# An embedding tower kernel: its first period gathered, turned, listed and contracted in two halves of 32 samples

## The chip, the core and the metric

The kernel runs on one core of a Trainium2 chip. The core has a matrix engine (TensorE, here PE, with a queue of its own for weight loads, PEld), a vector engine (VectorE, DVE), a scalar engine (ScalarE, ACT), GpSimd (POOL) and a queue engine for transfers (SyncE, SP). They run on their own instruction streams and meet at semaphores. The metric is the time of one execution on the device in microseconds (us).

## What is computed

For each of 1024 samples, 32 rows of 16 numbers are looked up in 32 tables (`x0`, fields m, components d). Three layers of a compressed interaction network follow, then a small dense tower:

```python
x0 = embeddings                      # [b, m, d], m = 32 fields, d = 16
xk = x0
outs = []
for W in (W0, W1, W2):               # W: [32, h, 64]
    xk = relu(einsum('bmd,bhd,mhk->bkd', x0, xk, W))
    outs.append(sum(xk, axis=2))
z = concatenate(outs, axis=1)        # [b, 192]
h = concatenate([z, dense_ctx], axis=1)
h = maximum(h @ W_top1 + b_top1, 0)
h = maximum(h @ W_top2 + b_top2, 0)
y = h @ W_top3
```

All numbers are fp32.

## The kernel before

**Tiles.** The batch is cut into 16 periods of 64 samples. A period has 64 x 16 = 1024 columns, cut into two streams of 512 columns (`s = 2q` and `2q + 1` of period q, the upper half of d in the second). Layers 1 and 2 multiply every field with every channel of the layer below: per stream and layer 16 steps of 128 rows, made in 4 units of 4 steps (`half` 0 or 1, `u` 0 or 1). A unit is one DVE product of 128x2048 (`outer` in `vector`, L555): rows of listed fields times the stream's relu'd sums, which lie in PSUM as `x1a`/`x1b` (layer 1) or `x2a`/`x2b` (layer 2; a for half 0, b for half 1). There are 32 streams x 2 layers x 4 = 256 units. PE contracts a unit against `w1` or `w2` into `acca` or `accb`. The products go through a ring of five buffers (`RING`), so unit n waits until unit n - 5 is contracted (`s_used`).

**Slots.** `streams(j)` names what shares slot j: slot 0 has layer 1 of streams 0 and 1, slot j layer 1 of stream j + 1 and layer 2 of stream j - 1. PE (`outer`, L639) contracts two units at a time, one in each half of its columns, into the two halves of one PSUM bank; `vector_units(j)` is DVE's order of the eight units.

**How a period comes in.** GpSimd gathers 16 times 128 table rows (`gather`, L417) into `emb`, two buffers in turn. PE turns them into `spread` (`turn_fields`, L599), ACT copies them to the 32 partitions of `field` (`fields_out`, L778), and SP writes 30 copies of groups of eight fields, in a fixed pattern, to `field_dram` (`list_fields`, L318, five transfers, pieces of 2 KB). From there SP reads `mates` (L326), for later periods `across` and `squares`, and `rows` (L346): partition p of tile t holds field number p + t of the list.

**Layer 0.** For periods 0 and 1 DVE makes five products of 128x1024 (`product0`, L536) into `prod0`, which has four places, so the fifth waits for PE's first contraction. From period 2 on GpSimd makes four (L435) and ACT squares the fields. PE contracts them into `acc0` (`layer0`, L605, L619); `SUM0` says after which pair (slot, i) that stands in PE's order. ACT copies `acc0` twice into `x1a` (`input1`, L783) and, with halves exchanged, in four pieces into `x1b` (L789); `input2` does so for `x2a` and `x2b` from the sums of layer 1. `z1`, `z2`, `z3` (L795) write relu'd sums for the reduction over d, which GpSimd does (`halve12`, `halve3`, L439 to L445).

**Fillers.** `keep_busy` (L612) issues matmuls whose result is not used, in front of PE work that follows a wait.

**What sets the order.** All orders are written by hand, one per engine: `FIELDS_AT`, `SUM0` and `TOWER_AT` place turnings, layer 0 and the dense tower between pairs on PE, and `stretches(q)` cuts GpSimd's gathers by how far PE has come.

## Time and profile before

| | |
|---|---|
| median of 3 runs | 638.52 us (638.24 to 638.60) |
| profiled execution, its own time | 638.18 us |
| its span in the trace | 636.4 us |
| DVE busy | 579.8 us |
| PE busy | 584.7 us |
| GpSimd busy | 444.7 us |
| ACT busy | 366.3 us |

The span runs from the first to the last instruction of the profiled execution; 1.8 us of its own time lie outside it. A timeline row gives start and duration of merged instructions of one kind and, in brackets, the idle time before them and what ended it. Intervals of DVE and ACT in a row of several are their union. Each fp32 matmul of the code appears as two records. In the chain that ended last DVE's `outer` has 51% of the span and PE's contraction of pairs 17%.

### The profile page before, as it was taken

The numbers are of one execution on the slowest core, as the hardware profiler recorded it, in microseconds if no ns is written. First come the engines' busy times: TensorE is split into PE (matmuls) and PEld (weight loads), VectorE is DVE, ScalarE is ACT, GpSimd is POOL, SyncE is SP. The second block draws the span as 40 slices with busy tenths as digits, with TensorE's granted clock in tenths as the row PEclk, the third lists the DMA queues.
The fourth block names the chain that finished last, engine by engine and source line by source line (L and its number), as shares of the span: only waits on it lengthen the run. The fifth ranks groups of instructions, "written<-read, shape, count | busy, mean of one in ns | idle before, by whom it ended". The sixth has DMA issues, their size and how long they took to land.

```text
span 636.4 us, 7868 instructions
## 1 busy us (share of the span) xinstructions
PE 584.7 (92%) x2896; PEld 209.6 (33%) x2896; DVE 579.8 (91%) x309; ACT 366.3 (58%) x607; POOL 444.7 (70%) x416
## 2 busy tenths in 40 slices
PE   0078899999898989999999999999999999999998
PEld 0023233333232323333334323333334323334355
DVE  1039899999999999999999999999999999999995
ACT  0006474767656565747676575747676575737551
POOL 6677787698888878886979688886989582703012
PEclk9999999999999999999999999999999999999999
DMA  6296598938293845749291846648391946600000
GB/s 172 46 323 143 231 231 257 326 64 295 73 262 129 220 188 123 286 75 334 49 302 62 222 185 147 263 95 314 59 320 38 238 166 150 257 4 1 1 2 1
DMA packets 31315, 105.83 MB, mean 166 GB/s; under 512 B 8774, under 2 KB 14028, under 8 KB 27052
## 3 DMA queue, kind: packets, MB, share of 16 engines
q1 hardware_dynamic: 23084, 103.21, 51.6%
q0 software_dynamic: 8192, 2.11, 2.5%
q8 instruction: 23, 0.38, 0.2%
q14 instruction: 16, 0.13, 0.1%
HBM read 89.56 MB, written 15.73 MB: 165 GB/s over the span
## 4 chain that ended last, share of the span: by engine, by line
DVE 52%; PE 26%; issue 12%; DMA 5%; POOL 2%; SPq 1%; ACT 1%; DVEq 0%; ACTq 0%
DVE prod L555 51%; PE accb L648 9%; PE acca L648 8%; DMA rows<-field_dram 3%; POOL emb L417 2%; PE spread L691 2%; PE acc L605 2%; DMA field_dram<-zb_field 1%; PE accb L669 1%; PE acc L669 1%; SPq L318 1%; DVE prod L536 1%; PE spread L686 1%; ACT zb_field L778 0%; PE spread L612 0%
## 5 line engine op out<-in xcount | busy, mean ns | idle before, releaser
L417 POOL DMA_INDIRECT emb<-in_table,idx x256 | 246.4, 963 | 79.8 <-issue 67.8
L648 PE MATMUL acca<-prod,w 128*64 128x512 f32 x1024 | 229.1, 594 | 2.5 <-DVE prod L555 1.7
L648 PE MATMUL accb<-prod,w 128*64 128x512 f32 x960 | 216.1, 596 | 10.6 <-DVE prod L555 10.6
L555 DVE TENSOR_TENSOR prod<-rows,x1a 128x2048 f32<-128x2048 f32 x64 | 145.7, 2278 | 4.9 <-ACT x1a L783 2.5
L555 DVE TENSOR_TENSOR prod<-rows,x1b 128x2048 f32<-128x2048 f32 (+1 forms) x65 | 145.7, 2245 | 2.0 <-PE accb L648 1.4
L555 DVE TENSOR_TENSOR prod<-rows,x2a 128x2048 f32<-128x2048 f32 x64 | 145.6, 2278 | 0.8 <-PE accb L648 0.8
L555 DVE TENSOR_TENSOR prod<-rows,x2b 128x2048 f32<-128x2048 f32 x64 | 145.6, 2277 | 0.0
L648 PEld LDWEIGHTS acca<-prod,w 128*64 128x64 f32 x1024 | 71.7, 137 | 144.6 <-issue 134.3
L648 PEld LDWEIGHTS accb<-prod,w 128*64 128x64 f32 x960 | 65.8, 137 | 153.0 <-issue 113.7
L435 POOL TENSOR_TENSOR prod<-rows,mates 128x1024 f32<-128x1024 f32 x42 | 99.3, 2382 | 6.8 <-DMA rows<-field_dram 6.6
L783 ACT ACTIVATE x1a<-acc 64x512 f32<-64x512 f32 x62 | 35.3, 570 | 114.6 <-PE acc L605 113.9
L439 POOL TENSOR_TENSOR zin<-zin 128x512 f32<-128x512 f32 (+1 forms) x24 | 30.5, 1270 | 74.4 <-ACT zin L795 74.1
L789 ACT ACTIVATE x1b<-acc 32x512 f32<-32x512 f32 x124 | 69.9, 564 | 5.3 <-DVE prod L555 3.5
L605 PE MATMUL acc<-prod,w 128*64 128x512 f32 x248 | 59.0, 594 | 0.3 <-DVE prod L536 0.2
L789 ACT ACTIVATE x2b<-acca 32x512 f32<-32x512 f32 x64 | 36.0, 563 | 21.7 <-DVE prod L555 21.1
L795 ACT ACTIVATE zin<-accb 64x512 f32<-64x512 f32 (+1 forms) x32 | 33.0, 1032 | 26.0 <-PE accb L648 22.8
L536 DVE TENSOR_TENSOR prod<-rows,mates 128x1024 f32<-128x1024 f32 x10 | 11.7, 1223 | 36.4 <-DMA rows<-field_dram 34.7
L795 ACT ACTIVATE zin<-acca 64x512 f32<-64x512 f32 x32 | 33.8, 1056 | 15.0 <-PE acca L648 14.6
L435 POOL TENSOR_TENSOR prod<-across,mates 128x1024 f32<-128x1024 f32 x14 | 33.3, 2381 | 12.8 <-issue 12.5
L778 ACT ACTIVATE zb_field<-spread 32x256 f32<-32x256 f32 x64 | 23.9, 374 | 25.0 <-PE spread L599 24.1
L599 PE MATMUL spread<-ident,emb 128*32 128x128 f32 x256 | 11.2, 294 | 26.2 <-DMA emb<-in_table,idx 26.2
L789 ACT ACTIVATE x2b<-accb 32x512 f32<-32x512 f32 x60 | 33.8, 562 | 0.9
(84 smaller groups left out, 309.3 us busy)
## 6 DMA issues: line engine op xcount, KB each, us to landing
rows<-field_dram SPq DMA_DIRECT2D x30, 2048.0 KB, 11.9
field_dram<-zb_field SPq DMA_DIRECT2D x32, 256.0 KB
mates<-field_dram SPq DMA_DIRECT2D x16, 512.0 KB, 4.4
across<-field_dram SPq DMA_DIRECT2D x56, 128.0 KB, 4.5
emb<-in_table,idx POOLq DMA_INDIRECT x256
field_dram<-zb_field SPq DMA_DIRECT2D x32, 128.0 KB
field_dram<-zb_field SPq DMA_DIRECT2D x16, 192.0 KB
rows<-field_dram SPq DMA_DIRECT2D x2, 1024.0 KB, 7.1
```

The costliest lines, as they stand in the source:

```text
L417: pool.indirect_dma_start(out=emb[q % EMBS][:, j * EMB:(j + 1) * EMB], out_offset=None, in_=table, in_offset=bass.IndirectOffsetOnAxis(ap= ...
L435: nc.gpsimd.tensor_tensor(prod0[:, k, :], other, mates[:, :], ALU.mult).then_inc(s_prod0p, 1)
L439: nc.gpsimd.tensor_tensor(by_d[:, :, 0:DH], by_d[:, :, 0:DH], by_d[:, :, DH:EMB], ALU.add).then_inc(s_eight, 1)
L536: nc.vector.tensor_tensor(prod0[:, place0(q, k), :], rows[:, slot(q, t), :], mates[:, :], ALU.mult).then_inc(s_prod0v, 1)
L555: nc.vector.tensor_tensor(prod[:, n % RING, t:t + count, :], rows[:, at + t:at + t + count, c * HALF:(c + 1) * HALF], xs, ALU.mult).then_i ...
L605: mm = nc.tensor.matmul(to[c * HID:(c + 1) * HID, :], w, operand[:, c * HALF:(c + 1) * HALF], start=first, stop=last)
L648: mm = nc.tensor.matmul(acc[j % 2][side * HID:(side + 1) * HID, :], (w1 if layer == 1 else w2)[:, step, :], prod[:, (made(layer, s, half, ...
L669: mm = nc.tensor.matmul(sums_alone(s)[c * HID:(c + 1) * HID, 0:PART], w2[:, step, :], prod[:, n % RING, i, c * PART:(c + 1) * PART], start ...
L778: last = nc.scalar.activation(by_d[:, d, :, :, :], turned[d * FIELDS:(d + 1) * FIELDS, :, :, :], ACT.Copy)
L783: last = nc.scalar.activation(to[h * HID:(h + 1) * HID, :], src, ACT.Relu)
L789: last = nc.scalar.activation(to[block * FIELDS:(block + 1) * FIELDS, :], src[of:of + FIELDS, :], ACT.Relu)
L795: return nc.scalar.activation(by_d[:, c * count:(c + 1) * count, :], src.rearrange("k (d b) -> k d b", b=BT), ACT.Relu)
```

## The change

Period 0 is processed as two halves of 32 samples; h is the half. The ids of period 0 are laid out on the host so that the first 8 gathers bring all fields of samples 0 to 31 and the next 8 those of samples 32 to 63. GpSimd issues the second 8 after the first turning.

- `turn_first(h)`, `fields_first(h)`, `list_first(h)`, `mates_first(h)`, `rows_of_half(h, g)` do per half what was done once. A half's list has the same 30 copies in 8 transfers of 3 or 4 copies each (`EIGHTS`), in pieces of 128 numbers (512 B); 4 are issued by SP and 4 by ACT.
- A stream of period 0 is now one half of the samples with all 16 d, still 512 columns. `product_first(h, k)` makes products of 128x512, `layer0_first` contracts them in pieces of 256 columns.
- The 16 units of period 0 (`FIRST_UNITS`) are contracted one stream at a time (`outer_alone`, eight matmuls of 256 columns), in this order, two units per name: (1,0) half 0, (1,0) half 1, (2,0) half 0, (1,1) half 0, (1,1) half 1, (2,0) half 1, (2,1) half 0, (2,1) half 1, where (layer, stream). The products of half 1's layer 0 stand after the first four.
- ACT's copies for period 0 go by 256 columns: `split_twice` has 4 instructions (before 2), `split_changed_over` 8 (before 4), `split_by_d` 2 per half.
- Slots 0 and 1 are gone. The products of period 1 follow the 16 units, then slot 2 holds layer 1 of streams 2 and 3, and slot 3 has the order that slot 1 had. Layer 0 of period 2 follows the last pair of slot 2 (before, after pairs 0 and 1 of it); that of period 3 stands one pair later in slot 4.
- The first add of table bases to the ids covers period 0 alone, a second the other periods.

```diff
+    FIRST = [(0, 2), (2, 3), (5, 3)]
+    FIRST_SLOT = 2
+    FIRST_UNITS = ([(1, 0, half, u) for half in range(2) for u in range(UNITS)] +
+                   [(2, 0, 0, u) for u in range(UNITS)] +
+                   [(1, 1, half, u) for half in range(2) for u in range(UNITS)] +
+                   [(2, 0, 1, u) for u in range(UNITS)] +
+                   [(2, 1, half, u) for half in range(2) for u in range(UNITS)])
...
-    for q in range(2, PERIODS):
-        SUM0[2 * q - 2, 0] = [(k, q) for k in range(3)]
-        SUM0[2 * q - 2, 1] = [(SQUARES, q), (L0 - 1, q)]
+        late = q == 3
+        SUM0[2 * q - 2, late] = [(k, q) for k in range(3)]
+        SUM0[2 * q - 2, 1 + late] = [(SQUARES, q), (L0 - 1, q)]
...
+        def list_eights(queue, h, odd):
+            for first, of, step, times in EIGHTS[odd::2]:
...
+                queue.dma_start(to, part).then_inc(s_listed_first[h], 16)
...
-            list_fields(0)
-            mates_in(0)
-            for g, (t, count) in enumerate(FIRST):
-                spread_rows(0, t, count, s_first[g])
+            for h in range(SPLITS):
+                list_first(h)
+                mates_first(h)
+                for g in range(len(FIRST)):
+                    rows_of_half(h, g)
...
             pool.wait_ge(s_at, 1)
-            gather_early(0)
-
+            gather(0, 0, FIRST_GATHERS)
             pool.wait_ge(s_turned, 1)
+            pool.wait_ge(s_turned, 1)
+            gather(0, FIRST_GATHERS, FIRST_GATHERS)
+            pool.wait_ge(s_turned, SPLITS)
+            pool.wait_ge(s_at, 2)
             gather_early(1)
...
+                if k >= RING0:
+                    dve.wait_ge(s_l0, h * STEPS0 + k - RING0 + 1)
...
             pe.wait_ge(s_ident, 1)
-            turn_fields(0, 0)
+            turn_first(0)
 
             pe.wait_ge(s_w12, 32)
-            pe.wait_ge(s_listed, len(LIST_PARTS) * 16)
-            keep_busy(acc[1][:, :], 5)
+            pe.wait_ge(s_listed_first[0], len(EIGHTS) * 16)
+            keep_busy(acc[1][:, :], 2)
+            turn_first(1)
+            keep_busy(acc[1][:, :], 2)
             pe.wait_ge(s_w0sum, 3)
-            for k in order0(0):
-                layer0(k, 0)
-            turn_fields(1, 0)
-
+            for k in range(EARLY):
+                layer0_first(k, 0)
+            for i, unit in enumerate(FIRST_UNITS):
+                outer_alone(*unit)
+                if i == 2 * UNITS - 1:
+                    for k in range(EARLY):
+                        layer0_first(k, 1)
+                if i == 3 * UNITS - 1:
+                    turn_fields(1, 0)
+            turn_fields(2, 0)
+            for k in order0(1):
+                layer0(k, 1)
...
+            fields_first(0)
+            fields_first(1)
+            first_input(1, 0, 0)
+            first_input(1, 0, 1)
+            first_z(0, 0)
+            first_input(2, 0, 0)
+            first_input(2, 0, 1)
+            first_input(1, 1, 0)
+            first_z(1, 0)
+            first_input(1, 1, 1)
             fields_out(1)
```

DVE's order at the start. `prod0<-rows,mates` are products of layer 0, `prod<-rows,x..` units of layers 1 and 2. Before:

```order
L536 TENSOR_TENSOR prod0<-rows,mates 128x1024 x5
L555 TENSOR_TENSOR prod<-rows,x1a 128x2048
L555 TENSOR_TENSOR prod<-rows,x2a 128x2048
L555 TENSOR_TENSOR prod<-rows,x1a 128x2048
L555 TENSOR_TENSOR prod<-rows,x2a 128x2048
L555 TENSOR_TENSOR prod<-rows,x1b 128x2048
L555 TENSOR_TENSOR prod<-rows,x2b 128x2048
L555 TENSOR_TENSOR prod<-rows,x1b 128x2048
L555 TENSOR_TENSOR prod<-rows,x2b 128x2048
L536 TENSOR_TENSOR prod0<-rows,mates 128x1024 x5
L555 TENSOR_TENSOR prod<-rows,x2a 128x2048 x2
```

And now:

```order
L603 TENSOR_TENSOR prod0<-rows,mates 128x512 x5
L638 TENSOR_TENSOR prod<-rows,x1a 128x2048 x2
L638 TENSOR_TENSOR prod<-rows,x1b 128x2048 x2
L603 TENSOR_TENSOR prod0<-rows,mates 128x512 x5
L638 TENSOR_TENSOR prod<-rows,x1a 128x2048 x2
L638 TENSOR_TENSOR prod<-rows,x2a 128x2048 x2
L638 TENSOR_TENSOR prod<-rows,x2b 128x2048 x2
L638 TENSOR_TENSOR prod<-rows,x1b 128x2048 x2
L638 TENSOR_TENSOR prod<-rows,x2a 128x2048 x2
L638 TENSOR_TENSOR prod<-rows,x2b 128x2048 x2
L612 TENSOR_TENSOR prod0<-rows,mates 128x1024 x5
L638 TENSOR_TENSOR prod<-rows,x1a 128x2048
```

The products of period 1 moved from behind 8 units to behind 16, and layer 1 of streams 2 and 3 (slot 2) follows them, where before layer 2 of stream 0 (slot 1) did.

PE's order in slot 4 and the start of slot 5, where layer 0 of period 3 stands (`acc<-prod,w` and `acc<-squares,w`; a pair is `acca` or `accb` x8; `spread<-ident,emb` is the turning of period 4). Before:

```order
L599 MATMUL spread<-ident,emb 32x128 x8
L648 MATMUL acca<-prod,w 64x512 x8
L605 MATMUL acc<-prod,w 64x512 x6
L648 MATMUL acca<-prod,w 64x512 x8
L619 MATMUL acc<-squares,w 64x512 x2
L605 MATMUL acc<-prod,w 64x512 x2
L648 MATMUL acca<-prod,w 64x512 x16
L648 MATMUL accb<-prod,w 64x512 x32
```

And now:

```order
L684 MATMUL spread<-ident,emb 32x128 x8
L759 MATMUL acca<-prod,w 64x512 x16
L700 MATMUL acc<-prod,w 64x512 x6
L759 MATMUL acca<-prod,w 64x512 x8
L730 MATMUL acc<-squares,w 64x512 x2
L700 MATMUL acc<-prod,w 64x512 x2
L759 MATMUL acca<-prod,w 64x512 x8
L759 MATMUL accb<-prod,w 64x512 x32
```

One more pair (x8) stands ahead of the layer 0 products, and one pair fewer behind them.

ACT's order at the start, now, with `x1a<-acc` the first input of layer 1 and `DMA field_dram<-zb_field` its share of the listing (before, ACT issued no transfer):

```order
L907 ACTIVATE zb_field<-spread 32x4x32 x4
L339 DMA field_dram<-zb_field 32x4x128 x2
L339 DMA field_dram<-zb_field 32x3x128
L339 DMA field_dram<-zb_field 32x4x128
L907 ACTIVATE zb_field<-spread 32x4x32 x4
L339 DMA field_dram<-zb_field 32x4x128 x2
L339 DMA field_dram<-zb_field 32x3x128
L339 DMA field_dram<-zb_field 32x4x128
L915 ACTIVATE x1a<-acc 64x256 x4
```

Both halves' copies and eight transfers stand ahead of the first `x1a`, where one set of copies did.

## Rows read from the trace of the kernel before

**Rows 1.** Page, part 1: busy us, instructions; part 2: granted clock, 40 slices, tenths.

```profile
PE 584.7 (92%) x2896; PEld 209.6 (33%) x2896; DVE 579.8 (91%) x309; ACT 366.3 (58%) x607; POOL 444.7 (70%) x416
...
PEclk9999999999999999999999999999999999999999
```

**Rows 2.** Timeline of DVE: start us, us, line, operation, count [idle before].

```profile
40.87 5.98 DVE L536 TENSOR_TENSOR prod<-rows,mates 128x1024 f32<-128x1024 f32 x5 [33.95 <-DMA rows<-field_dram]
49.32 2.29 DVE L555 TENSOR_TENSOR prod<-rows,x1a 128x2048 f32<-128x2048 f32 x1 [2.46 <-ACT x1a L783]
51.52 2.28 DVE L555 TENSOR_TENSOR prod<-rows,x2a 128x2048 f32<-128x2048 f32 x1
...
68.58 4.63 DVE L536 TENSOR_TENSOR prod<-rows,mates 128x1024 f32<-128x1024 f32 x4 [1.59 <-issue]
74.00 1.22 DVE L536 TENSOR_TENSOR prod<-rows,mates 128x1024 f32<-128x1024 f32 x1 [0.79 <-DMA rows<-field_dram]
```

**Rows 3.** Timeline of GpSimd (POOL), 0 to 100 us.

```profile
3.67 1.12 POOL L417 DMA_INDIRECT emb<-in_table,idx  x1 [2.20 <-DVE idx L514]
...
22.59 0.94 POOL L417 DMA_INDIRECT emb<-in_table,idx  x1 [0.30 <-issue]
26.32 0.94 POOL L417 DMA_INDIRECT emb<-in_table,idx  x1 [2.79 <-PE spread L599]
...
98.37 7.07 POOL L435 TENSOR_TENSOR prod<-rows,mates 128x1024 f32<-128x1024 f32 x3 [2.88 <-DMA rows<-field_dram]
```

**Rows 4.** Timeline of PE, 0 to 50 us.

```profile
24.94 1.09 PE L599 MATMUL spread<-ident,emb 128*32 128x128 f32 x16 [24.94 <-DMA emb<-in_table,idx]
34.46 7.04 PE L612 MATMUL accb<-w 128*128 128x512 f32 x10 [8.44 <-DMA field_dram<-zb_field]
...
49.87 4.56 PE L612 MATMUL accb<-w 128*128 128x512 f32 x10
```

**Rows 5.** Timeline of ACT, 20 to 75 us.

```profile
26.08 1.53 ACT L778 ACTIVATE zb_field<-spread 32x256 f32<-32x256 f32 x4 [24.05 <-PE spread L599]
48.04 1.15 ACT L783 ACTIVATE x1a<-acc 64x512 f32<-64x512 f32 x2 [20.43 <-PE acc L605]
...
70.79 1.15 ACT L783 ACTIVATE x2a<-acca 64x512 f32<-64x512 f32 x2 [12.10 <-PE acca L648]
```

**Rows 6.** Timeline of SP's queue, 25 to 55 us.

```profile
27.63 3.90 SPq L318 DMA_DIRECT2D field_dram<-zb_field  x5
34.34 0.34 SPq L326 DMA_DIRECT2D mates<-field_dram  x1
...
51.95 3.88 SPq L318 DMA_DIRECT2D field_dram<-zb_field  x5
```

**Rows 7.** DMA, 28.5 to 30.5 us: queue: packets, MB, share of 16 engines' time.

```profile
q1 hardware_dynamic: 210, 0.40, 99.6%
```

**Rows 8.** Page, part 3: queue, packets, MB, share of 16 engines' span.

```profile
q0 software_dynamic: 8192, 2.11, 2.5%
```

**Rows 9.** DMA, 34.5 to 47 us: totals.

```profile
DMA packets 896, 4.49 MB, mean 360 GB/s; under 512 B 167, under 2 KB 279, under 8 KB 535
```

**Rows 10.** Groups by shape, 560 to 637 us: xcount | busy, mean ns.

```profile
L669 PE MATMUL accb<-prod,w 128*64 128x256 f32 x64 | 7.3, 381 | 0.0
...
L795 ACT ACTIVATE zin<-accb 64x256 f32<-64x256 f32 x2 | 1.2, 610 | 2.8 <-PE accb L669 2.8
```

**Rows 11.** Timeline of DVE, 75 to 160 us.

```profile
98.80 2.29 DVE L555 TENSOR_TENSOR prod<-rows,x2a 128x2048 f32<-128x2048 f32 x1 [0.84 <-PE accb L648]
...
111.99 2.28 DVE L555 TENSOR_TENSOR prod<-rows,x2a 128x2048 f32<-128x2048 f32 x1
...
151.61 2.28 DVE L555 TENSOR_TENSOR prod<-rows,x2a 128x2048 f32<-128x2048 f32 x1
```

**Rows 12.** Timeline of PE, one pair of units in slot 4.

```profile
140.22 3.60 PE L648 MATMUL acca<-prod,w 128*64 128x512 f32 x16
```

**Rows 13.** Timeline of ACT, 140 to 150 us.

```profile
145.65 1.15 ACT L783 ACTIVATE x1a<-acc 64x512 f32<-64x512 f32 x2 [6.64 <-PE acc L605]
```

More of the change, by code:

```diff
@@ L70, in cin_tower_kernel @@
     BLOCKS = P // FIELDS
+    SPLITS = 2
+    SPLIT = BT // SPLITS
+    FIRST_GATHERS = GATHERS // SPLITS
+    PIECE = QUAD * SPLIT
+    EIGHTS = [(first + e, 2 * half + j // 8 + e, step, times) for j, count, half, first, step, times in LIST_PARTS
+              for e in range(count // 8)]
     GROUPS = [(0, 4), (4, 4)]
-    FIRST = [(0, 2), (2, 2), (4, 1), (5, 3)]
+    FIRST = [(0, 2), (2, 3), (5, 3)]
     BUFFERS = 3
@@ L741, in _ @@
             pe.wait_ge(s_ctx, 16)
-            towers, turned = 0, 2
-            for j in range(SUBS):
+            towers, turned = 0, turned_by(2)
+            for j in range(FIRST_SLOT, SUBS):
                 for i in range(2 * UNITS if j < SUBS - 1 else 4 * UNITS):
@@ L747, in _ @@
                     else:
[L748 to L751 removed]
+                        outer_alone(*vector_units(j)[i])
                     if (j, i) in TOWER_AT:
@@ L779, in fields_out, with fields_first @@
                 last.then_inc(s_field, 1)
+            def fields_first(h):
+                act.wait_ge(s_turned, h + 1)
+                by_d = field[:, h * HALF:(h + 1) * HALF].rearrange("n (f d b) -> n d f b", f=BLOCKS, b=SPLIT)
+                turned = spread[:, h * P:(h + 1) * P].rearrange("q (f b) -> q f b", b=SPLIT)
+                for d in range(QUAD):
+                    last = nc.scalar.activation(by_d[:, d, :, :], turned[d * FIELDS:(d + 1) * FIELDS, :, :], ACT.Copy)
+                last.then_inc(s_field, 1)
+                act.wait_ge(s_field, h + 1)
+                list_eights(act, h, 1)
@@ new lines, in split_by_d, with layer0_half @@
+            def split_by_d(to, of, h, done):
+                by_d = to.rearrange("k (b d) -> k d b", d=EMB)
+                for c in range(2):
+                    last = nc.scalar.activation(by_d[:, c * DH:(c + 1) * DH, h * SPLIT:(h + 1) * SPLIT],
+                                                of[c * HID:(c + 1) * HID, :].rearrange("k (d b) -> k d b", b=SPLIT), ACT.Relu)
+                last.then_inc(done, 1)
+            def layer0_half(h):
+                return acc0[:, h * PART:(h + 1) * PART]
```

317 lines of the change are left out of this document (218 added, 99 removed).

## The prediction

> **What bounds the kernel now.** I read the page first: DVE is busy for 579.8 us of the 636.4 us span and PE for 584.7 us [rows 1]. In steady state one `outer` unit starts 2.20 us after the one before it (49.32 to 51.52) [rows 2], and there are 256 of them, which makes 563 us. A pair of units costs PE 3.60 us [rows 12] against 4.40 us on DVE, so DVE sets the pace. What an edit at the start can bring is therefore the idle time of DVE before and between its first units. The timeline of DVE shows it: nothing until 40.87 us, five products of layer 0, 2.46 us of waiting for `x1a`, the eight units of slot 0, then the products of period 1 at 68.58 us, the last of which waits for rows until 74.00 us [rows 2].
>
> The timelines of the other engines show what the first 40.87 us are made of, in series: 16 gathers from 3.67 to 22.59 us, 1.26 us apart [rows 3]; 2.35 us from the start of the last to the turning on PE, which takes 1.09 us [rows 4]; four copies by ACT, 1.53 us [rows 5]; the listing, 27.63 to 34.34 us [rows 6]; then 6.5 us until mates and the first rows are in [rows 2, 6]. The change attacks this series.
>
> **What comes earlier: half 0.** Eight gathers at 1.26 us put the eighth at 12.5 us, and 2.35 us later PE turns it: 14.8 us. It has half the matmuls, so half of 1.09 us: 15.4 us. ACT then copies 32x128 pieces in place of 32x256 (383 ns each) [rows 5]; between half of that and all of it I take 0.31 us, four of them 1.3 us: 16.7 us.
>
> The listing of a half is 960 pieces of 512 B in place of 480 of 2 KB for the whole. The wire time is the unknown. In the listing of before, 210 packets fill 16 engines to 99.6% for 2 us, so one takes 152 ns, and the rate is 0.2 MB per us [rows 7]. If bytes decide, 0.49 MB take 2.5 us. If each piece costs what a packet of 2 KB does, 960 x 152 / 16 = 9.1 us. The gathers' packets of about 258 B cost 2.5% of 16 x 636.4 us over 8192 packets, 31 ns each [rows 8], which is far nearer the first. I take 3.0 us. The listing of before has 6.7 us from issue to mates, of which 0.98 MB at that rate are 4.9 us, so 1.8 us lie around it: a half lands 4.8 us after its fields, at 21.5 us. Two issuing queues, SP's and ACT's, are not counted as a gain, since the engines were full.
>
> That full wire agrees with the Trainium skill, DMA: Bandwidth & Descriptors, Rules for kernel authors: spreading transfers over SP, ACT and GpSimd doesn't add bandwidth and only saves issue time. The same page's Specifications give 512 B as the smallest transfer at line rate; by that the pieces would take the 2.5 us and the sum would be 0.5 us better, and no run here shows pieces of 512 B from SBUF yet.
>
> Mates and first rows are half the bytes: 0.75 MB less at 360 GB/s [rows 9] is 2.1 us off the 6.5 us: 25.9 us, against 40.87 us.
>
> **What holds half 0 back again: half 1.** PE's queue has `turn_first(1)` and two groups of two `keep_busy` matmuls ahead of the first contraction. GpSimd's second eight gathers start only after the first turning: 15.4 + 0.3 = 15.7 us, the eighth at 24.5 us, turned at 26.8 to 27.4 us. The second `keep_busy` pair takes 1.8 us at the rate of the later group (4.56 us for five) [rows 4]; the first group ran five in 7.04 us, and its slow ones are at half that rate [rows 4], which would make a pair 3.6 us. The granted clock is listed as full (9, 90% or more) in every slice [rows 1], so the durations are what I go by. PE idles from 25 to 27 us here, so either is possible. The fifth product of layer 0 waits for the first contraction (`prod0` has four places). So contractions end at 31.4 us at the fast rate and 33.9 us at the slow one; I take 32.4 us, between them.
>
> ACT splits each field by 256 columns: four `ACTIVATE` at 383 ns [rows 5] are 1.6 us for `x1a` (1.15 us before), and eight are 3.1 us for `x1b` (2.3 us before). So `x1a` is ready at 34.0 us and the first unit starts at 34.1 us, 15.2 us earlier than 49.32 us. ACT's own four DMA issues of half 1 lie at 28.7 us to 30.5 us (SP's first ones of before take about 0.4 us, all five 3.90 us because the wire was full [rows 6]), before it is needed.
>
> **From there to period 1.** DVE runs 4 units (34.1 to 42.9), five half products (3.0 us; the rows of half 1 would be in at about 37 us, so nothing is waited for), then waits about 0.6 us for layer 2 of half 0: PE ends the fourth unit 1.8 us after it is made (64 records of 128x256 in 7.3 us are four units) [rows 10], and ACT needs 1.6 us. The twelve units left are 26.4 us with 0.2 us of waiting for ACT: 73.1 us. The rows of period 1 don't come earlier in proportion: ACT copies the fields of period 1 only after `first_input(1, 1, 1)`, ending at 56.9 us. From the start of that listing (51.95) to the first product was 16.6 us, to the fifth 22.0 us [rows 2, 6], so 73.6 and 79.0 us; the fifth product ends at 80.3 us. Now 16 units are done where before 8 were (at 75.2 us): 17.6 us of units for 5.1 us.
>
> **What is uncovered.** Two hand-overs that had cover lose it. First, slot 2 starts right after these products, so DVE waits 2.4 us for the last contraction and `x1a`, as it did once before [rows 2]: 82.7 us. Eight units later, at 100.3 us, DVE needs `x2a` of stream (2, 2), for which PE must finish the pair (3.65 us) and ACT copy twice (1.15 us). Before, DVE ended slot 0 at 66.99 us and ACT ended `x2a` at 71.94 us [rows 2, 5], and the products of period 1 lay in that gap. Now nothing does: 4.9 us idle, until 105.2 us. That is unit 25; before it started at 111.99 us [rows 11]. Gain so far 6.8 us.
>
> Then unit order a, a, b, b on slot 3 makes the ring of five wait twice, which before fell into slots 1 and 2 (0.84 us the longer [rows 11]): 1.3 us. Last, layer 0 of period 3 stands one pair later on PE. Before, it ended at 145.6 us and `x1a` at 146.8 us [rows 13], for the second unit of slot 5, which is the one before that at 151.61 us [rows 11] and so starts at 149.4 us: 2.6 us of margin. One pair costs 3.6 us on PE [rows 12]; with the backlog of the wait before it `x1a` comes at 145.8 us where DVE wants it at 143.9 us: 1.9 us. Unit 43 starts at 105.2 + 18 x 2.198 + 1.3 + 1.9 = 148.0 us, before at 151.61 us [rows 11]: 3.6 us. Later slots keep their order, so this stays to the end.
>
> GpSimd is 1.4 us late after gather(1) (27.7 against 26.32 [rows 3]), which doesn't count: its products of period 2 were held by rows until 98.37 us [rows 3], those rows are asked for about 2 us earlier now, so they end near 103.5 us (105.44 before), and PE takes them up from 103.9 us, wanting the last only at 107 us. Extra adds and memsets on DVE (32 memsets took 0.9 us) lie under the gathers.
>
> Sum against the profiled execution: 638.18 - 3.6 = 634.6 us; the median is 0.34 us above it, so 634.9 us.
>
> **Rivals.** (1) *The late pieces don't bite*: `keep_busy` at the fast rate (0.9 us), and period 3's `x1a` in time (1.9 us), wire by bytes (0.5 us): 6.9 us gained, 631.6 us. For it: each term stands on margins of 1 to 2 us. Against: they would all have to fall the same way.
>
> (2) *The head start is eaten*: PE at its slow rate past 27 us (1.5 us more), first units slow as well because PE idles some 4 us before them (0.5 us), and period 1's rows 1 to 2 us later: 3.5 us less, 638.4 us, no change. For it: the group at 34.46 us started slow after idling [rows 4].
>
> (3) *ACT is blocked by its own listing, slower*: if a piece costs 152 ns, half 0 lands at 27.6 us, and PE's turning of half 1 moves behind it to 31.8 us. Half 1's wire takes 9.1 us from 33.1 us, and ACT's four issues are held as SP's were (3.90 us of issuing for 4.9 us of wire [rows 6, 7]), until about 40.4 us; `first_input(1, 0, 0)` is queued behind them. The first unit then starts at 42.0 us, 7.9 us later than forecast: 642.8 us. It turns slower once the first unit starts after 37.7 us, that is at about 110 ns a piece. Against: 31 ns for the gathers' packets.
>
> (4) *The split doesn't advance the first unit*, since everything waits for PE's order: then the first unit would be near 49 us. The sum above would need 15 us of error; it would give some 650 us and has 0.01, counted in (3).
>
> **Numbers.** Forecast 0.60, from 1.3 to 6 us gained. Rival 1 has 0.08, rival 2 0.16, rival 3 with 4 0.16. A measurement of this kernel can tell about 0.2%, 1.3 us, from no change. Faster 0.68, same 0.16, slower 0.16. The range leaves out most of rival 3 and the far end of rival 1: 631.0 to 639.0 us.
>
> **What would show it.** First product of layer 0 at about 26 us and first unit at 34.1 us; period 1's products at 73.6 us with the fifth at 79.0 us; 4.9 us of DVE idle before the first `x2a` unit of slot 3; about 1.9 us before the second unit of slot 5; unit 43 at 148.0 us. I am wrong if a half's listing takes over 6 us, if PE's contractions end after 35 us, or if the products of GpSimd for period 2 or 3 are what PE waits for.

## The result

The changed kernel takes 642.40 us (median of 6 runs, 640.50 to 642.99) beside 638.58 us before (6 runs, 638.24 to 638.93): the ratio is 1.0053 (95% interval 1.0039 to 1.0067). It is slower by 0.5%, where 634.9 us and a gain were forecast. The profiled execution took 640.72 us with a span of 638.8 us, against 638.18 and 636.4 us before.

The granted clock of the changed kernel in 40 slices, in tenths. Before, this line was full throughout [rows 1].

```profile
PEclk9889999899999999999999999999999999999999
```

Timeline of DVE, the changed kernel. It answers to [rows 2, 11]. Units are counted in DVE's order: unit 25 is the first of slot 3, unit 43 the third of slot 5.

```profile
25.10 1.29 DVE L603 TENSOR_TENSOR prod<-rows,mates 128x512 f32<-128x512 f32 x2 [17.60 <-DMA rows<-field_dram]
...
35.84 0.69 DVE L603 TENSOR_TENSOR prod<-rows,mates 128x512 f32<-128x512 f32 x1 [5.11 <-PE acc L721]
39.16 4.49 DVE L638 TENSOR_TENSOR prod<-rows,x1a 128x2048 f32<-128x2048 f32 x2 [2.63 <-ACT x1a L915]
...
78.39 5.87 DVE L612 TENSOR_TENSOR prod<-rows,mates 128x1024 f32<-128x1024 f32 x5
86.87 2.29 DVE L638 TENSOR_TENSOR prod<-rows,x1a 128x2048 f32<-128x2048 f32 x1 [2.61 <-issue]
...
109.48 4.48 DVE L638 TENSOR_TENSOR prod<-rows,x2a 128x2048 f32<-128x2048 f32 x2 [4.94 <-ACT x2a L961]
...
121.62 2.29 DVE L638 TENSOR_TENSOR prod<-rows,x2b 128x2048 f32<-128x2048 f32 x1 [1.06 <-PE accb L759]
125.13 4.49 DVE L638 TENSOR_TENSOR prod<-rows,x1b 128x2048 f32<-128x2048 f32 x2 [1.21 <-PE accb L759]
...
134.60 2.29 DVE L638 TENSOR_TENSOR prod<-rows,x2a 128x2048 f32<-128x2048 f32 x1 [0.60 <-PE accb L759]
...
151.87 2.29 DVE L638 TENSOR_TENSOR prod<-rows,x1a 128x2048 f32<-128x2048 f32 x1 [1.79 <-ACT x1a L961]
154.07 2.28 DVE L638 TENSOR_TENSOR prod<-rows,x2a 128x2048 f32<-128x2048 f32 x1
```

The first product comes 15.8 us earlier than before (25.10 against 40.87), the first unit 10.2 us earlier (39.16 against 49.32), unit 25 is 2.5 us ahead (109.48 against 111.99), and unit 43 is 2.46 us behind (154.07 against 151.61). From there both kernels run alike: 2.4 us is also the difference of the spans (638.8 against 636.4). So everything that decides lies in the first 154 us.

SP's queue and, below it, GpSimd and PE of the changed kernel (start us, us, operation, count, idle before).

```profile
16.51 1.79 SPq L339 DMA_DIRECT2D field_dram<-zb_field  x4
20.84 0.34 SPq L366 DMA_DIRECT2D mates<-field_dram  x1
21.23 1.39 SPq L371 DMA_DIRECT2D rows<-field_dram  x3
```

```profile
24.86 0.94 POOL L470 DMA_INDIRECT emb<-in_table,idx  x1 [0.30 <-issue]
32.21 0.94 POOL L470 DMA_INDIRECT emb<-in_table,idx  x1 [6.40 <-PE spread L694]
```

```profile
20.96 3.68 PE L707 MATMUL accb<-w 128*128 128x512 f32 x4 [5.63 <-DMA field_dram<-zb_field]
31.25 0.67 PE L694 MATMUL spread<-ident,emb 128*32 128x128 f32 x8 [6.61 <-DMA emb<-in_table,idx]
31.84 3.37 PE L707 MATMUL accb<-w 128*128 128x512 f32 x4
...
41.51 8.79 PE L784 MATMUL acca<-prod,w 128*64 128x256 f32 x64 [3.98 <-DVE prod L638]
...
116.23 8.78 PE L759 MATMUL accb<-prod,w 128*64 128x512 f32 x32 [3.69 <-DVE prod L638]
127.47 7.09 PE L759 MATMUL accb<-prod,w 128*64 128x512 f32 x32 [2.46 <-DVE prod L638]
```

The listing of a half is quick, 16.51 to 20.84 us, with the 16 DMA engines busy with its pieces for 84.7% of the time (17 to 20 us: totals, then SP's queue q1 and ACT's q10):

```profile
DMA packets 1059, 0.47 MB, mean 157 GB/s; under 512 B 141, under 2 KB 1059, under 8 KB 1059
...
q1 hardware_dynamic: 544, 0.25, 45.5%
q10 hardware_dynamic: 456, 0.21, 39.2%
```

The rows of half 0 are then asked for at 21.23 us. The last gather of half 1 starts at 24.86 us, near the 24.5 us of the forecast, and is turned only at 31.25 us. The chain of waits gives the time between to that one transfer, and a third of it to the last gather of half 0, beside which no other kind of transfer ran:

```profile
12.38 2.15 DMA emb<-in_table,idx
...
24.86 6.25 DMA emb<-in_table,idx
```

The transfers of 25 to 28 us: totals, then packets, MB and share of 16 engines of SP's queue (q1, the rows) and GpSimd's (q0, the gathers):

```profile
DMA packets 197, 0.95 MB, mean 317 GB/s; under 512 B 25, under 2 KB 44, under 8 KB 197
...
q1 hardware_dynamic: 164, 0.94, 83.4%
q0 software_dynamic: 33, 0.01, 5.6%
```

The rows take most of the engines' time, and the gathers' small packets (q0) trickle among them. Stretches of the changed kernel (busy us and count of PE, PEld, DVE, ACT, POOL, then granted clock, DMA share, GB/s):

```profile
26.00:32.00 6.00, 0.75 (x9) 0.40 (x9) 1.69 (x3) 0.03 (x1) 0.00 (x0) 0.65 0.53 198
32.00:36.00 4.00, 4.00 (x12) 1.65 (x14) 0.16 (x1) 1.04 (x4) 2.88 (x4) 0.67 0.52 94
42.00:46.00 4.00, 4.00 (x26) 2.35 (x24) 4.00 (x3) 1.17 (x2) 3.09 (x4) 0.64 0.71 263
...
116.00:120.00 4.00, 3.77 (x10) 1.18 (x12) 4.00 (x3) 3.89 (x7) 3.09 (x4) 0.57 1.15 227
```

The clock goes to its lower level, 1.2 of 2.4 GHz, around three idle stretches of PE, 24.6 to 31.2 us, 37.5 to 41.5 and 112.5 to 116.2 us: in steps of 2 us the granted clock is 0.50 in every step from 28 to 34 us, at 42 to 44 and at 118 to 120 us. Not every idle stretch is followed by it: behind 2.46 us of idling, at 127.47 us, the clock is full and 32 records take 7.09 us. And the column doesn't show all slow work: the four records at 20.96 us took 3.68 us, twice the 1.8 us of the full rate, with a granted clock of 1.00 in every step from 20 to 26 us. The idle stretch from 112.5 us lies between layer 0 of period 2, now behind the last pair of slot 2, and the first `x2a` unit of slot 3.

### The profile page after: what moved, and what is told of

Its sections match the earlier page's. It is cut to its first block, busy times and chain, and to the rows that moved or that the text cites. A ratio compares the mean times of both kernels' runs of the same rounds, so it can differ in the third digit from the quotient of the medians.

```text
span 638.8 us, 8220 instructions
## 1 busy us (share of the span) xinstructions
PE 581.9 (91%) x3026; PEld 218.3 (34%) x3026; DVE 581.6 (91%) x347; ACT 371.1 (58%) x641; POOL 443.2 (69%) x416
## 4 chain that ended last, share of the span: by engine, by line
DVE 49%; PE 33%; issue 12%; POOL 2%; ACT 2%; DMA 2%; DVEq 1%; ACTq 0%; POOLq 0%
DVE prod L638 49%; PE accb L759 10%; PE acca L759 9%; PE acc L700 3%; PE acca L784 3%; POOL emb L470 2%; PE spread L806 2%; DMA emb<-in_table,idx 1%; PE accb L784 1%; PE acc L784 1%; PE acc L730 1%; PE accb L707 1%; PE spread L801 1%; DVEq L627 0%; ACT x2b L923 0%
## 5 line engine op out<-in xcount | busy, mean ns | idle before, releaser
L759 PE MATMUL acca<-prod,w 128*64 128x512 f32 x960 | 215.0, 594 | 4.1 <-DVE prod L638 3.3
L759 PE MATMUL accb<-prod,w 128*64 128x512 f32 x896 | 203.3, 600 | 15.5 <-DVE prod L638 15.5
L759 PEld LDWEIGHTS acca<-prod,w 128*64 128x64 f32 x960 | 67.2, 137 | 137.0 <-issue 127.0
L759 PEld LDWEIGHTS accb<-prod,w 128*64 128x64 f32 x896 | 61.9, 137 | 149.6 <-issue 107.2
L492 POOL TENSOR_TENSOR zin<-zin 128x512 f32<-128x512 f32 (+1 forms) x24 | 30.5, 1270 | 77.5 <-ACT zin L973 77.2
L967 ACT ACTIVATE x1b<-acc 32x512 f32<-32x512 f32 x116 | 65.4, 564 | 4.7 <-DVE prod L638 3.0
L700 PE MATMUL acc<-prod,w 128*64 128x512 f32 x236 | 55.6, 592 | 0.0
L967 ACT ACTIVATE x2b<-acca 32x512 f32<-32x512 f32 x60 | 33.8, 563 | 16.4 <-DVE prod L638 15.8
L973 ACT ACTIVATE zin<-acc 64x512 f32<-64x512 f32 x30 | 31.8, 1058 | 0.5
L967 ACT ACTIVATE x2b<-accb 32x512 f32<-32x512 f32 x56 | 31.5, 562 | 0.8
L603 DVE TENSOR_TENSOR prod<-rows,mates 128x512 f32<-128x512 f32 x10 | 6.5, 686 | 26.1 <-DMA rows<-field_dram 20.6
```

What stands on the lines that cost most here:

```text
L492: nc.gpsimd.tensor_tensor(by_d[:, :, 0:DH], by_d[:, :, 0:DH], by_d[:, :, DH:EMB], ALU.add).then_inc(s_eight, 1)
L700: mm = nc.tensor.matmul(to[c * HID:(c + 1) * HID, :], w, operand[:, c * HALF:(c + 1) * HALF], start=first, stop=last)
L759: mm = nc.tensor.matmul(acc[j % 2][side * HID:(side + 1) * HID, :], (w1 if layer == 1 else w2)[:, step, :], prod[:, (made(layer, s, half, ...
L967: last = nc.scalar.activation(to[block * FIELDS:(block + 1) * FIELDS, :], src[of:of + FIELDS, :], ACT.Relu)
L973: return nc.scalar.activation(by_d[:, c * count:(c + 1) * count, :], src.rearrange("k (d b) -> k d b", b=BT), ACT.Relu)
```

## The experiments

All ratios are to the kernel before, run on the same chip beside it.

**Theory.** The rows of half 0 delay the last gather of half 1 by 4 us; PE's clock after its idle stretches costs 1.6 us at the start and more in slots 3 and 4; and layer 0 of period 3 costs 1.8 us in slot 5. **Rivals:** GpSimd's waits for the turnings delay it; PE's order alone does; or GpSimd's late gathers of period 1 do.

### The changed kernel again

> The changed kernel once more, unchanged. Theory A (PE's clock falls in three idle stretches, and how long it stays low depends on the moment at which the stretch falls): the time is again between 640.5 and 643.0 us, and this profile shows the same three stretches under full clock (about 26 to 36 us, 42 to 46 us, 116 to 120 us), with durations that differ by some tenths to 2 us. Theory B (the scatter of 2 us between runs comes from the transfers at the start): the first unit on DVE starts at another time than 39.16 us while the clock columns stay the same.

641.15 us (5 runs, 640.61 to 645.47), ratio 1.0043 (1.0029 to 1.0058). The profiled execution was the slowest one, 645.47 us, which is 2.5 us above the range expected, and so shows what scatters. Timelines of DVE and PE in it (the last row of PE, as in a later profile too, counts only the records up to the end of the window asked for):

```profile
85.16 1.23 DVE L612 TENSOR_TENSOR prod<-rows,mates 128x1024 f32<-128x1024 f32 x1 [1.85 <-DMA rows<-field_dram]
...
124.75 2.29 DVE L638 TENSOR_TENSOR prod<-rows,x2b 128x2048 f32<-128x2048 f32 x1 [2.18 <-PE accb L759]
```

```profile
118.22 9.90 PE L759 MATMUL accb<-prod,w 128*64 128x512 f32 x32 [3.69 <-DVE prod L638]
130.59 4.92 PE L759 MATMUL accb<-prod,w 128*64 128x512 f32 x14 [2.46 <-DVE prod L638]
```

The first unit is at 39.26 us, as in the other profile. The 4.7 us between the two executions are 1.85 us of rows of period 1 that came late, and 5.6 us of ring waits (2.18 + 1.21 + 1.13 + 1.08) in place of 2.9: the first 32 records of slot 3 take 9.90 us, or 8.78 in the other profile, and the next 32, behind the 2.46 us of idling, are slow here too (granted clock 0.50 at 132 to 134 us) where they ran at the full rate in the other.

### Rows of half 0 held back

```diff
                 for g in range(len(FIRST)):
+                    if (h, g) == (0, 1):
+                        sp.wait_ge(s_turned, SPLITS)
                     rows_of_half(h, g)
```

> SP issues row groups 2 and 3 of half 0 only after half 1 is turned; nothing else differs. Theory A (the gathers of half 1 land late, 6.4 us after the last issue in place of 2.3 us, because half 0's rows fill the 16 engines): half 1 is turned at 27 to 28.5 us in place of 31.25 us. Rival (the gather after a wait lands late by itself, whatever else is under way): it is still turned at about 31 us. The first unit does not gain as much, since rows now come later: 35 to 38 us in place of 39.16 us, and the whole 0 to 3 us faster than the changed kernel.

640.61 us (10 runs), ratio 1.0024 (1.0004 to 1.0044). PE's timeline:

```profile
27.61 0.66 PE L696 MATMUL spread<-ident,emb 128*32 128x128 f32 x8 [3.15 <-DMA emb<-in_table,idx]
```

The turning comes at 27.61 us, 3.6 us earlier, and 0.2 to 0.8 us behind the forecast of 26.8 to 27.4. The chain gives 2.35 us to the last gather, from 25.12 us, in place of 6.25. With nothing else changed ahead of it, the rows' traffic is shown to be the cause. The held rows cost part of it again (they made DVE wait 5.83 us, first unit at 37.23 us).

### No waits of GpSimd for the turnings

```diff
             gather(0, 0, FIRST_GATHERS)
-            pool.wait_ge(s_turned, 1)
-            pool.wait_ge(s_turned, 1)
             gather(0, FIRST_GATHERS, FIRST_GATHERS)
-            pool.wait_ge(s_turned, SPLITS)
             pool.wait_ge(s_at, 2)
             gather_early(1)
```

Each half has a semaphore of its own for its gathers here.

> GpSimd waits for no turning in periods 0 and 1: the second eight gathers follow the first at once, and those of period 1 follow them; the halves have semaphores of their own, so that the buffers are safe. Theory A (half 1's gathers land late because they fall into half 0's rows, and they fall there because of the wait of 2.8 us): the last one starts at about 22.3 us in place of 24.86 us, half 1 is turned at 24.7 to 28 us in place of 31.25 us, the first unit starts at 32.5 to 36 us, and GpSimd is 8 us ahead at the gathers of period 1. The kernel is 3 to 5 us faster than the changed one. Rival (the wait was covered, the rows alone decide): turned at 30 us or later, the first unit at 38 to 39 us, under 1.5 us faster.

640.39 us (9 runs), ratio 1.0024 (1.0008 to 1.0040). The sixteen gathers now go out 1.25 us apart without a gap, the last at 22.63 us, 2.2 us earlier. PE's timeline:

```profile
30.23 0.66 PE L692 MATMUL spread<-ident,emb 128*32 128x128 f32 x8 [5.15 <-DMA emb<-in_table,idx]
```

The turning moves by 1.0 us and the first unit to 38.25 us, as the rival had it. The last gather now takes 7.46 us to land: of the 2.2 us that GpSimd saves, 1.2 us are lost in the same traffic. The wait named in the change is a small part of the cost.

### Only the wait before the gathers of period 1 removed

```diff
             gather(0, FIRST_GATHERS, FIRST_GATHERS)
-            pool.wait_ge(s_turned, SPLITS)
```

> Only the wait of GpSimd for the second turning is gone; period 1's gathers start at 26.1 us in place of 32.2 us. Theory A (GpSimd is not what the end waits for in the changed kernel): unit 25 still starts at 109 to 110 us, time within 0.5 us of the changed kernel. Rival (the lateness of 6 us on GpSimd is what eats the head start): period 1's rows and the later products come sooner and the kernel is 2 us or more faster.

644.21 us (3 runs, 642.95 to 644.95), ratio 1.0083 (1.0062 to 1.0103): no gain. The first unit is at 39.06 us and the turning at 31.18 us, as in the changed kernel, and the profile is like the slower one of the changed kernel (rows of period 1 late by 1.92 us, ring waits of 5.4 us). The expectation, within 0.5 us of the changed kernel, was missed by more than 1 us on the slow side; the run's interval overlaps the changed kernel's first (1.0039 to 1.0067) and not the second (1.0029 to 1.0058), so with three runs a real loss is not settled. SP asks for the listing of period 1 at 61.84 us here and at 61.95 us in the changed kernel. So GpSimd, 5.9 us late at `gather_early(1)` (32.21 against 26.32 [rows 3]), is not what the end waits for in this order.

### PE kept busy until half 1 is there

```diff
-            keep_busy(acc[1][:, :], 2)
+            keep_busy(acc[1][:, :], 8)
             turn_first(1)
```

> Eight keep_busy matmuls in place of two ahead of the turning of half 1, where PE idled for 6.6 us. Theory A (PE came out of that idle time at half rate): the two after the turning take 1.8 us in place of 3.4 us, contractions follow at 33.7 us in place of 35.1 us, first unit at about 37.6 us, and the kernel is 1.0 to 1.6 us faster than the changed one. Rival (the rate there does not matter since rows or the fifth product decide): first unit unchanged at 39.2 us.

639.02 us (10 runs, 637.46 to 641.77), ratio 1.0016 (1.0001 to 1.0032). PE's timeline:

```profile
21.14 9.09 PE L707 MATMUL accb<-w 128*128 128x512 f32 x16 [5.45 <-DMA field_dram<-zb_field]
30.74 0.46 PE L694 MATMUL spread<-ident,emb 128*32 128x128 f32 x8 [0.51 <-DMA emb<-in_table,idx]
31.13 1.98 PE L707 MATMUL accb<-w 128*128 128x512 f32 x4
```

The turning is nearly as late as ever, but the four records behind it take 1.98 us in place of 3.37, and the first unit starts at 37.06 us, 2.1 us earlier. Of these, 0.5 us are the turning itself, as this execution's last gather landed in 5.38 us; 1.6 us are what the slow records and the slow turning behind the idle stretch cost.

### Half 1 turned behind the contraction of half 0

```diff
-            keep_busy(acc[1][:, :], 2)
-            turn_first(1)
-            keep_busy(acc[1][:, :], 2)
+            keep_busy(acc[1][:, :], 4)
             pe.wait_ge(s_w0sum, 3)
             for k in range(EARLY):
                 layer0_first(k, 0)
+            turn_first(1)
...
             fields_first(0)
-            fields_first(1)
             first_input(1, 0, 0)
+            fields_first(1)
```

> PE turns half 1 behind the contractions of half 0 in place of ahead of them, with the four keep_busy in one group, and ACT copies half 1's fields after the first x1a. Theory A (half 0 was held back by half 1's gathers through PE's order alone): contractions start on their products, the first unit starts at 33 to 34.5 us in place of 39.16 us, and the start of half 1 is not later than before (turned at 31 to 33 us). If all of it stays, the kernel is 4 to 5 us faster than the changed one, 637.5 to 638.5 us. Rival (the rows of half 0, late for the same traffic, decide as well): first unit at 36 us or later.

638.63 us (10 runs), ratio 1.0004 (0.9992 to 1.0016). The first unit starts at 33.35 us, 5.8 us before that of the changed kernel and 0.75 us before the forecast, and slot 3 at 107.47 us, only 2.0 us before it. The time is 2.5 to 3.8 us below the changed kernel's two medians; 4 to 5 us were expected if all of the start stayed. DVE, then PE:

```profile
33.35 4.49 DVE L638 TENSOR_TENSOR prod<-rows,x1a 128x2048 f32<-128x2048 f32 x2 [2.35 <-ACT x1a L914]
39.18 4.49 DVE L638 TENSOR_TENSOR prod<-rows,x1b 128x2048 f32<-128x2048 f32 x2 [1.34 <-ACT x1b L922]
...
80.20 1.23 DVE L612 TENSOR_TENSOR prod<-rows,mates 128x1024 f32<-128x1024 f32 x1 [1.26 <-PE acc L700]
```

```profile
78.40 0.68 PE L684 MATMUL spread<-ident,emb 128*32 128x128 f32 x16 [2.06 <-DMA emb<-in_table,idx]
```

ACT's copies and transfers of half 1 now stand ahead of `x1b` (1.34 us), the rows of half 1 come late (1.15 us), and the turning of period 2, which stands ahead of period 1's contraction in PE's order, waits for GpSimd until 78.40 us. So the fifth product of period 1 waits 1.26 us and `x1a` of slot 2 makes DVE wait 3.43 us in place of 2.61. Here GpSimd's lateness does count, once the start is 6 us faster.

### PE kept busy ahead of slot 3

```diff
                     for k, q in SUM0.get((j, i), []):
                         layer0(k, q)
+                    if (j, i) == (FIRST_SLOT, 3):
+                        pe.wait_ge(s_field, turned)
+                        keep_busy(spread[:, :], 4)
```

> Four keep_busy matmuls behind layer 0 of period 2, where PE idled for 3.7 us ahead of the first pair of slot 3. Theory A (that idle time let PE's clock fall and the slow pairs cost DVE waits at the ring): the clock column is full from 112 to 128 us, the first two pairs take 7.1 us in place of 8.8 us, the waits of DVE in slots 3 and 4 add up to 1.3 us in place of 2.9 us (5.6 us in e1_again), and the kernel is 1.5 to 2.5 us faster than the changed one, with less scatter. Rival (the ring waits come from the unit order alone): no change in them.

640.75 us (9 runs), ratio 1.0031 (1.0017 to 1.0045). PE's timeline and a stretch of this kernel:

```profile
118.76 7.09 PE L759 MATMUL accb<-prod,w 128*64 128x512 f32 x32
128.31 3.97 PE L759 MATMUL accb<-prod,w 128*64 128x512 f32 x10 [2.46 <-DVE prod L638]
```

```profile
128.00:132.00 4.00, 3.69 (x10) 1.15 (x12) 4.00 (x3) 3.38 (x7) 3.69 (x3) 0.57 0.89 346
```

The pairs behind the filled gap run in 7.09 us, at the full rate, but the clock falls again behind the next idle stretch, 2.46 us in the middle of slot 3. The ring waits are 2.8 us, no less than in the first profile of the changed kernel: half of the expectation held. The scatter didn't shrink either (639.28 to 643.12 us).

### Layer 0 of period 3 where it stood

```diff
-        late = q == 3
+        late = False
```

> Layer 0 of period 3 stands where it stood before, after pairs 0 and 1 of slot 4. Theory A (PE's order costs 1.8 us, since x1a of slot 5 comes late): the wait of 1.79 us ahead of the second unit of slot 5 is gone and nothing takes its place, as GpSimd's products end at 136.4 us and pair 0 at 138.7 us; 1.8 us faster than the changed kernel. Rival (GpSimd is late there and PE would wait for it): PE waits in front of layer 0, DVE waits at the ring, gain under 0.5 us.

640.93 us (5 runs, 640.32 to 641.76), ratio 1.0032 (1.0017 to 1.0047). The wait of 1.79 us in slot 5 is gone, and nothing stands in its place. Against the changed kernel the times overlap, but the profile adds up: against that of the changed kernel its first unit is 0.8 us later and its rows of period 1 are 1.85 us late, and yet its span is only 0.5 us longer. The run with the fills, below, sizes it.

### All idle stretches filled

```diff
-            keep_busy(acc[1][:, :], 2)
+            keep_busy(acc[1][:, :], 8)
             turn_first(1)
...
                 layer0_first(k, 0)
+            keep_busy(acc[1][:, :], 4)
...
+                    if (j, i) in ((FIRST_SLOT, 3), (FIRST_SLOT + 1, 1)):
+                        pe.wait_ge(s_field, turned)
+                        keep_busy(spread[:, :], 4 if j == FIRST_SLOT else 3)
```

> All idle stretches of TensorE that the split opened are filled with products on data already there, nothing else is changed: 8 in place of 2 before the turning of half 1, 4 after half 0's contraction, 4 after layer 0 of period 2 in slot 3 and 3 in the middle of the next slot. Theory (behind the late turning, the rest of the loss is TensorE's clock after idle stretches): the turning of half 1 stays at 30.7 to 31.3 us, but the products behind it run at full rate, the first unit starts at 36.5 to 37.1 us, the granted clock is 1.00 from 32 us to the end of slot 4, the ring waits of slots 3 and 4 are together 1.3 to 1.8 us (2.9 and 5.6 in the two profiled runs of the changed kernel), the wait for x1a in slot 5 stays at 1.8, the span is about 635.5 and the time 636.5 to 637.5, with under 1.5 us between the fastest and the slowest. Rival (the scatter comes from DMA landings or the ring itself): ring waits of 2.5 us and more at a full clock, time 639 to 641 and a scatter as before.

638.19 us (10 runs, 637.22 to 638.69), ratio 0.9991 (0.9981 to 1.0001). The granted clock is full in every run, the turning comes at 30.70 us and the first unit at 37.02 us, as expected, and DVE's timeline has ring waits of 1.5 us in slots 3 and 4:

```profile
121.79 4.49 DVE L638 TENSOR_TENSOR prod<-rows,x1b 128x2048 f32<-128x2048 f32 x2 [0.67 <-PE accb L759]
...
131.51 2.29 DVE L638 TENSOR_TENSOR prod<-rows,x2a 128x2048 f32<-128x2048 f32 x1 [0.84 <-PE accb L759]
```

That is the 1.3 us of the forecast, nearly. Six of the eleven runs of the changed kernel took over 642 us; here the slowest took 638.69 and the spread is 1.5 us. The medians are 3.0 and 4.2 us below those of the changed kernel, or 3.3 and 4.0 us by the ratios, and this is what the slow work behind the idle stretches costs. Against the kernel before nothing is gained: the interval holds 1. The time is 0.7 us above what was expected; 0.90 us of waiting for rows of period 1 stand in this profile.

### The fills, with layer 0 of period 3 where it stood

The two edits above together.

> The same fills, and the layer 0 of period 3 placed behind pairs 0 and 1 of its slot, where it stood before the change (it stood behind pairs 1 and 2 in the changed kernel). Theory: the 1.8 us wait for x1a at the start of slot 5 goes and nothing takes its place, so the time is 1.5 to 2 us below that of the fills alone: 634.5 to 635.8. Rival: VectorE meets the ring or the next x2a instead, and the time is that of the fills alone within 0.5 us.

636.40 us (6 runs, 635.10 to 637.39), ratio 0.9965 (0.9953 to 0.9978): 1.8 us less than the fills alone, which is the length of the wait of 1.79 us. The median lies 0.6 us above the expected range, as with the fills alone. DVE's second unit of slot 5 starts without a wait:

```profile
147.18 2.29 DVE L638 TENSOR_TENSOR prod<-rows,x1a 128x2048 f32<-128x2048 f32 x1
```

### All of it, with half 1 turned behind the contraction

The slot fills, layer 0 of period 3 where it stood, the order of "Half 1 turned behind the contraction of half 0" with four fillers behind that turning, and no wait ahead of `gather_early(1)`, the gathers of period 1 (the expectation calls them those of period 2).

> The fills in the slots and the early layer 0 of period 3 again, and half 1 turned only behind the contraction of half 0 (4 filling products behind the turning), its fields copied by ScalarE behind the first x1a, and no wait of GpSimd before the gathers of period 2. Theory: the first unit starts at 33.3 to 33.8 us, some 3 us before that of the fills alone; of it 1.3 us is given back to the wait for x1b, 1.2 to the rows of half 1, and the 3.4 us wait for x1a of slot 2 that stood in the run with the turning behind the contraction shrinks by about 1 us as GpSimd no longer holds the turning of period 2; unit 43 starts at 148 to 149.5 and the time is 633 to 635.5. Rival: the waits for x1b, rows and the fifth product take all that the earlier first unit gives, and the time is that of the fills with the early layer 0 within 0.5 us.

632.62 us (4 runs, 631.79 to 635.80), ratio 0.9918 (0.9888 to 0.9949): faster than both kernels, and 0.4 us below the range expected, as the rows of half 1 made DVE wait for only 0.27 us. DVE:

```profile
33.56 4.49 DVE L637 TENSOR_TENSOR prod<-rows,x1a 128x2048 f32<-128x2048 f32 x2 [2.35 <-ACT x1a L917]
...
82.47 2.29 DVE L637 TENSOR_TENSOR prod<-rows,x1a 128x2048 f32<-128x2048 f32 x1 [2.61 <-ACT x1a L963]
...
105.08 4.49 DVE L637 TENSOR_TENSOR prod<-rows,x2a 128x2048 f32<-128x2048 f32 x2 [4.94 <-ACT x2a L963]
...
146.40 2.28 DVE L637 TENSOR_TENSOR prod<-rows,x2a 128x2048 f32<-128x2048 f32 x1
```

Unit 25 starts at 105.08 us, where the forecast had 105.2, and unit 43 at 146.40 us, 1.6 us ahead of the 148 expected for this run, which is 5.2 us before 151.61 [rows 11]; the spans differ by the same 5.2 us (631.2 against 636.4). The wait for `x1b` remains (1.37 us). The wait of the fifth product of period 1 (1.26 us) is gone, and the one for `x1a` of slot 2 is down from 3.43 us, in the run with the turning behind the contraction, to 2.61 us, with GpSimd no longer held. Which of the four edits gives how much beyond the run before was not taken apart further.

## Why the prediction was wrong

The direction was wrong, and 642.4 us lies outside the range of 631 to 639 us. One of the signs that the prediction named for being wrong came up: PE's contractions ended after 35 us. In its own steps, against the profiled execution of the changed kernel:

| step | forecast | measured |
|---|---|---|
| listing of a half, from its fields | 4.8 us | 16.5 to 20.8, 4.3 us |
| first product | 25.9 | 25.10 |
| half 1 turned | 26.8 to 27.4 | 31.25 |
| four records of `keep_busy` behind it | 1.8 (slow: 3.6) | 3.37 |
| contractions end | 32.4 | 37.5 |
| first unit | 34.1 | 39.16 |
| wait for `x1a` of slot 2 | 2.4 | 2.61 |
| idle before `x2a` of slot 3 | 4.9 | 4.94 |
| unit 25 | 105.2 | 109.48 |
| ring waits in slots 3 and 4 | 1.3 | 2.9 (5.6 in the second profile) |
| late `x1a` of slot 5 | 1.9 | 1.79 |
| unit 43 | 148.0 | 154.07 |

**The step that failed** is the turning of half 1. The prediction put "the eighth at 24.5 us, turned at 26.8 to 27.4 us": it took the 2.35 us between a gather and its turning from rows beside which only gathers ran [rows 3, 4]. The gathers of half 1 land while the rows of half 0 fill the engines, which its own text had at 360 GB/s [rows 9], and the last took 6.25 us. In the seven profiles with these rows under way it took 5.4 to 7.5 us. Holding the rows brought the turning to 27.61 us; starting the gathers 2.2 us earlier brought it only to 30.23. The prediction's rule on the wire agreed with its page and was applied to the listing alone. The Trainium skill, DMA: Bandwidth & Descriptors, Issuing engines are not separate DMA queues, says that transfers of SyncE, ScalarE and GpSimd run on the same 16 engines and interleave with each other; the 6.25 us against 2.15 us agree with it and give it a size.

**The second** is PE's rate. The end of the contractions was put between the fast and the slow rate. A wait of 2 us for half 1 was foreseen and one of 6.6 us came, and the slow rate with it, which the filled start sized at 1.6 us against the full rate. Of these two steps together come the 5.1 us at the first unit; 0.8 us are given back until unit 25, since the rows of period 1 made DVE wait for nothing in this execution. That is in part luck: in the second profile they cost 1.85 us.

**The third** is the ring. "1.3 us" was taken from the pairs of before at the full clock. The prediction saw that layer 0 of period 2 goes behind slot 2 and that DVE idles for 4.9 us before slot 3, but not that PE then idles for 3.7 us there, and for 2.5 us in the middle of slot 3. Slot 3 has slot 1's order now, and before, five and three fillers stood at these two places of slot 1; the change has none there. PE before:

```profile
76.89 4.56 PE L612 MATMUL accb<-w 128*128 128x512 f32 x10
...
88.89 2.84 PE L612 MATMUL spread<-w 128*128 128x512 f32 x6
```

This is 1.6 us here and 4.3 in the second profile; with the gaps filled the ring waits were 1.5 us, near the size that was forecast. Of the 4.7 us between the two profiled executions the ring has 2.7.

The sum closes: 4.3 us at unit 25, 1.6 us of ring, 0.2 us of the rest are the 6.1 us by which unit 43 is late, and 634.6 + 6.1 is 640.7 us, the profiled execution's 640.72. The median is 1.7 us higher, and where that lies is not shown, since no execution near it was profiled: the ring and the rows of period 1 are what differs between the two profiles, but the granted clocks of the six runs, 0.987 to 0.992, don't follow their times.

**What held.** The bytes decide the listing: a half takes 4.3 us, near the forecast, where 9.1 us of wire stood at the other end. The Trainium skill, DMA: Bandwidth & Descriptors, Specifications, gives 512 B as the smallest transfer at line rate; the trace nearly agrees: 157 GB/s from 17 to 20 us, the ramp included, are a fifth less than the 0.2 MB per us of the 2 KB pieces [rows 7], but the engines were busy for 84.7% of it, and a piece took 41 ns of one engine where a quarter of the 152 ns is 38. By an estimate from this, 960 pieces are 2.5 us of wire, and with the forecast's 1.8 us around it the 4.3 us are explained. The prediction's term of 3.0 us was 0.5 us too long. Also right were both uncovered hand-overs, and the late layer 0 of period 3, which the runs with and without it size at 1.8 us. The head start was about as good as the prediction said once the turning was out of the way and the gaps were filled: unit 25 at 105.08 us. The closeness to 105.2 is in part luck: a wait of 1.37 us for `x1b` that the forecast lacked is made up by a first unit 0.5 us earlier and by rows of period 1 that came in time.

**The rivals.** Rival 3 gave 642.8 us, but the time agrees and the mechanism doesn't: a piece costs about 41 ns of one engine, a quarter of the 152 ns, and ACT's four issues took 1.84 us. Rival 2, the head start eaten by PE's slow rate and slow first units, had the right mechanism for part of the loss, at 638.4 us; it had the landing of half 1 in neither its price nor its reasons. It was also to leave no change, and lacked a term for slots 3 and 4. A rival with the gathers behind the rows' traffic was missing, though both its rows were there. The remark on GpSimd held for this order, but not by its reasons: it was late by 5.9 us and not 1.4, the rows of period 2 were asked for 3.8 us later (93.02 against 89.26 us) and not 2 earlier, and its products ended at 109.45 us, not 103.5, which was still in time for PE. With the turning behind the contraction the remark no longer holds.

**What stays open.** Why the rows of period 1 make DVE wait between 0 and 1.9 us, from execution to execution (0, 1.85, 1.92 us in three profiles whose first units start within 0.2 us of each other), was not tried; how much of the scatter at a full clock it is, is not shown. Nor is it known why the same 2.46 us of idling is followed by slow work in some executions and not in others. The time of the last kernel rests on four runs with one of them at 635.8 us.

## What to carry to other kernels

When a loading phase is split so that its second half overlaps the first half's bulk transfers, price each small transfer of the second half at its landing time under that traffic, and put nothing that waits for it ahead of the first half's work on an in-order engine. A change that removes or moves pairs on TensorE also moves its idle stretches: list each idle stretch that it leaves, and fill it or price the work behind it at half the clock. A head start is worth what is left of it at the first point where all orders are again the old ones; compute that point, and check every hand-over that lay under the work that was moved.

## What the runs showed of the hardware

- An indirect gather of 128 rows landed 2.15 us after its start with only gathers under way, and 6.25 us after it with row transfers beside it (317 GB/s in all). Over seven profiles with these rows it was 5.4 to 7.5 us, and 2.35 us with them held back.
- Pieces of 512 B from SBUF to HBM, issued by two queues, moved at 157 GB/s: 1000 packets of the two queues took 84.7% of 16 engines' 3 us, 41 ns of one engine each. Pieces of 2 KB take 152 ns [rows 7].
- Idle stretches of TensorE of 6.6, 4.0 and 3.7 us were each followed by work in stretches whose mean granted clock was 0.57 to 0.67, between the two levels. A stretch of 2.46 us was followed by slow work in four of nine profiles (32 records in 8.5 to 8.8 us) and by work at the full rate in five (7.09 us).
- How long the clock stays low differs between executions of the same kernel: behind the same 3.7 us of idling 32 records took 8.78 or 9.90 us, and 7.09 us with the gap filled.
- The fastest and slowest run of the changed kernel lay 2.5 us apart in six runs and 4.9 us in five, those of the kernel before 0.7 us in six runs and 0.7 to 1.8 us in three larger sets. With all gaps filled it was 1.5 us in ten runs and, with layer 0 of period 3 moved as well, 2.3 us in six, all at a full clock: the clock is not the only thing that scatters.
- A granted clock of 1.00 in the profile doesn't prove the full rate: the first four records of the changed kernel took 0.92 us each under it, and 0.46 us is the full rate.
